# DLRM tower on one core: ACT's relu of an outer-product round in two halves, with the copies of the turned rows between them

## The chip, the cores and the metric

The kernel runs on one core of one Trainium2 chip. The metric is the device time of one launch in microseconds (us), the median of several runs. Engines are named as in the profile: PE (TensorE, matmuls; PEld are its weight loads), DVE (VectorE), ACT (ScalarE), POOL (GpSimd), SP (SyncE, which here only issues DMAs).

## The reference, cut to what matters

Sixteen table rows of 256 numbers are gathered for each of 2048 samples (`e`). Three layers follow. Each forms all products of field f of the embeddings with field g of the layer's own input, contracts the 256 pairs with weights over the 256 columns, adds a bias, applies relu and sums. In the layers k = 1 and 2 the second factor is the same number in every column, so it is an outer product of a projection of the embeddings with the 16 sums of the layer ahead.

```python
for i in range(3):
    z = einsum('bfe,bge->bfge', x, xk).reshape(B, 256, E).swapaxes(1, 2)
    z = einsum('bcl,oc->bol', z, Ws[i]) + bs[i][None, :, None]
    z = sum(relu(z), axis=-1)          # 16 numbers a sample
    outs.append(z)
    xk = broadcast_to(z[:, :, None], (B, F, E))
h = concatenate([*outs, dense_ctx], axis=1)
y = relu(relu(h @ W_top1 + b_top1) @ W_top2 + b_top2) @ W_top3
```

## The kernel before

The batch is cut into 256 tiles of 8 samples x 16 fields, taken two at a time: 128 **slots**. Eight slots make a **group** of 128 samples; there are 16 groups. I write p0 to p7 for a slot's number modulo 8. The slots 12 to 15 are p4 to p7 of the first round of the pattern, and from slot 20 on every eight slots are alike.

In each slot s every engine does this, in an order written out by hand:

- POOL gathers the rows of slot s+4 (two indirect DMAs) and multiplies small parts of the products of slot s+1.
- PE transposes the rows of slot s+2 into PSUM (`turn`, L653; it waits for the DVE products of slot s), then sums the products of slot s with the weights (`sum_pairs`, L675), then does what the slot has beside that: a projection (p3, L753), an **outer round** (p4, p5 for k=0, p0, p1 for k=1; L743), a **fold** (p6 for k=0, p3 for k=1; L774), or parts of the final layers.
- ACT copies the turned rows of slot s+2 from PSUM to SBUF (`take_turned`, two copies, L489 and L490), takes relu and a sum of slot s's pairs (`relu_pairs`, L517 and L521), and squares the fields of slot s+2 (L507).
- DVE multiplies the shifted fields of slot s (`products`, L232; it waits for ACT's two copies of slot s, made two slots earlier), and in p3 it adds relu of the second round of k=1 (L389), in p4 it transposes the projection and reduces a fold, in p0 it reduces the other fold, in p1 the pairs' sums.

An outer round is four matmuls j = 0 to 3 that fill the four banks of `outer_ps`, 128 x 2048 numbers. ACT turns a round into `relu_k` with one instruction over all four banks (`relu_round`, L528), at the head of the slot after the round, ahead of the copies. Of the two rounds q = 0 and 1 of k=1 DVE takes the second. The next round may not write `outer_ps` before that, so PE waits on `outer_relu` ahead of the round q = 1. The fold sums `relu_k` over fields: for k=0 the 16 matmuls of round q = 0 and the 16 of q = 1 (each shown as two passes in the trace, so 64), behind one wait for the relu of q = 1; it writes bank 0 (k=0) or 1 (k=1) of `outer_ps`.

The 16 sums of layer 0 pass through DRAM: ACT's copy (L542, p2), four small writes and one read of 256 KB on SP's queue (L265, L269) into `z_wide`. PE waits for that read inside `sum_pairs` of p4, three matmuls before its end, ahead of the outer round.

## Time and profile before

| | us |
|---|---|
| median of 3 runs (572.27 to 573.78) | 572.27 |
| the profiled execution | 569.55 |
| its span | 567.6 |
| one group of eight slots in the steady part | 33.23 |

The profile gives for each engine its busy time, for each instruction its start and length, and for each idle stretch what ended it. A start and the start of the next instruction on the same engine are the safer pair: lengths on ACT and DVE overlap by a tenth or so of a microsecond, and the ends of matmuls are modelled.

### The profile page before, as it was taken

How to read it: one execution, taken by the hardware profiler on the slowest of the kernel's cores; microseconds unless marked ns; L12 is line 12 of the kernel's file. 1: busy time of each engine (PE TensorE's matmuls, PEld its weight loads, DVE VectorE, ACT ScalarE, POOL GpSimd, SP SyncE). 2: the span in 40 equal slices, each digit the busy share in tenths (PEclk: the TensorE clock that was granted, in tenths of full speed). 3: DMA queues.
4: the chain of work that ended last, by engine and by line, in shares of the span. 5: the costliest groups of instructions: out<-in, count | busy, mean ns of one | idle time of the engine just before them, and what ended most of it. 6: DMA issues, size and time to landing. Idle time of an engine off the chain costs nothing.

```text
span 567.6 us, 17941 instructions
## 1 busy us (share of the span) xinstructions
PE 533.4 (94%) x7520; PEld 302.9 (53%) x7520; DVE 524.3 (92%) x257; ACT 408.5 (72%) x1219; POOL 458.4 (81%) x547
## 2 busy tenths in 40 slices
PE   2776999999999999999999999999999999999997
PEld 1433454555556555554655555555555555555466
DVE  4899899999999999999999999999999999999853
ACT  3566775868878686786868778786877868687743
POOL 6898999998989889897898979888897988988100
PEclk9999999999999999999999999999999999999999
DMA  3622323232232323223232322323222232322000
GB/s 89 176 69 73 86 68 89 65 93 63 64 84 68 85 59 92 60 67 86 58 94 58 83 70 65 83 63 91 61 71 79 61 86 66 86 59 71 14 2 2
DMA packets 27969, 40.57 MB, mean 71 GB/s; under 512 B 16880, under 2 KB 17264, under 8 KB 27888
## 3 DMA queue, kind: packets, MB, share of 16 engines
q0 software_dynamic: 12288, 33.57, 20.8%
q1 hardware_dynamic: 15600, 5.86, 4.2%
q8 instruction: 58, 0.95, 0.7%
q14 instruction: 23, 0.19, 0.1%
HBM read 38.75 MB, written 0.66 MB: 69 GB/s over the span
## 4 chain that ended last, share of the span: by engine, by line
ACT 32%; PE 28%; DVE 17%; issue 14%; POOL 6%; DMA 2%; SPq 0%; ACTq 0%; DVEq 0%; POOLq 0%
ACT relu_k L528 13%; PE sum_ps L675 12%; DVE prods L232 11%; ACT relu L517 6%; DVE relu_k L389 5%; PE outer_ps L774 5%; ACT prods L507 4%; POOL emb L285 4%; PE turn_ps L653 3%; ACT emb_t L489 3%; ACT h L559 2%; PE sum_ps L690 2%; ACT own L521 2%; POOL prods L298 1%; PE outer_ps L743 1%
## 5 line engine op out<-in xcount | busy, mean ns | idle before, releaser
L232 DVE TENSOR_TENSOR prods<-turn_ps,emb_t 128x3248 f32<-128x3248 f32 (+2 forms) x126 | 447.9, 3572 | 11.9 <-ACT emb_t L490 11.8
L285 POOL DMA_INDIRECT emb<-tables,rows_sb x256 | 252.0, 984 | 44.2 <-issue 38.0
L675 PE MATMUL sum_ps<-prods,w_sb 128*32 128x272 f32 x4096 | 264.8, 397 | 3.0 <-POOL prods L232 2.7
L675 PEld LDWEIGHTS sum_ps<-prods,w_sb 128*32 128x32 f32 x4096 | 121.3, 110 | 100.0 <-issue 13.3
L517 ACT ACTIVATE relu<-sum_ps,bias_twice 128x120 f32<-128x120 f32 x256 | 92.8, 378 | 96.5 <-PE sum_ps L675 96.4
L298 POOL TENSOR_TENSOR prods<-emb_t 128x256 f32<-128x256 f32 x128 | 95.2, 744 | 29.2 <-ACT emb_t L490 27.2
L489 ACT COPY emb_t<-turn_ps 128x512 f32<-128x512 f32 (+1 forms) x126 | 76.4, 606 | 36.5 <-PE turn_ps L653 36.4
L653 PEld LDWEIGHTS turn_ps<-ident_sb,emb 128*128 128x128 f32 x502 | 53.0, 141 | 74.2 <-DVE prods L232 53.3
L653 PE MATMUL turn_ps<-ident_sb,emb 128*128 128x128 f32 x502 | 83.2, 288 | 9.6 <-DVE prods L232 7.8
L232 POOL TENSOR_TENSOR prods<-emb_t 128x224 f32<-128x224 f32 (+1 forms) x128 | 89.9, 703 | 2.3
L528 ACT ACTIVATE relu_k<-outer_ps,bias_k 128x2048 f32<-128x2048 f32 x44 | 88.3, 2006 | 0.3 <-PE outer_ps L743 0.3
L507 ACT ACTIVATE prods<-emb_t 128x512 f32<-128x512 f32 x128 | 84.8, 663 | 0.2
L743 PE MATMUL outer_ps<-z_wide,proj_b 32*128 32x512 f32 x488 | 70.1, 643 | 1.2 <-DVE relu_k L421 0.6
L517 ACT ACTIVATION_READ_ACCUMULATOR relu<-sum_ps,bias_twice 128x1 f32 x256 | 55.8, 218 | 0.0
L774 PEld LDWEIGHTS outer_ps<-relu_k,fold_sb 128*32 128x32 f32 x1536 | 41.7, 110 | 20.5 <-ACT relu_k L528 10.7
L774 PE MATMUL outer_ps<-relu_k,fold_sb 128*32 128x128 f32 x1536 | 48.0, 274 | 4.0 <-ACT relu_k L528 3.7
L490 ACT COPY emb_t<-turn_ps 128x256 f32<-128x256 f32 (+1 forms) x126 | 51.6, 409 | 0.0
L521 ACT ACTIVATE own<-sum_ps,bias_sb 128x32 f32<-128x32 f32 x128 | 39.5, 309 | 0.0
L743 PEld LDWEIGHTS outer_ps<-z_wide,proj_b 32*128 32x128 f32 x488 | 20.0, 190 | 27.8 <-issue 19.5
L389 DVE SCALAR_TENSOR_TENSOR relu_k<-outer_ps,bias_less,relu_k 128x2048 f32<-128x2048 f32 x14 | 32.8, 2342 | 0.0
L753 PE MATMUL outer_ps<-emb_t,wp_sb 128*32 128x512 f32 x256 | 30.5, 592 | 0.0
L690 PE MATMUL sum_ps<-h,w_sb 128*128 128x128 f32 x216 | 28.6, 275 | 0.0
(81 smaller groups left out, 249.4 us busy)
## 6 DMA issues: line engine op xcount, KB each, us to landing
emb<-tables,rows_sb POOLq DMA_INDIRECT x256, 2.8
z_wide<-z_spread SPq DMA_DIRECT2D x15, 256.0 KB, 2.7
z_spread<-z_cat SPq DMA_DIRECT2D x60, 2.0 KB, 1.7
w_sb<-w_top SPq DMA_DIRECT2D x1, 512.0 KB
z_spread<-z_wide SPq DMA_DIRECT2D x2, 256.0 KB
w_sb<-w_top SPq DMA_DIRECT2D x1, 256.0 KB
ids_sb<-ids_t SPq DMA_DIRECT2D x1, 129.0 KB, 2.0
z_cat<-dense_b SPq DMA_DIRECT2D x1, 128.0 KB
```

The source lines that it names most:

```text
L232: eng.tensor_tensor(out, every, shifted, ALU.mult).then_inc(done, 1)
L285: nc.gpsimd.indirect_dma_start(out=emb[:, k % EMB_RING, t * E:(t + 1) * E], out_offset=None, in_=tables, in_offset=bass.IndirectOffsetOnAx ...
L298: nc.gpsimd.tensor_tensor(prod_blocks(k)[:, :, SHIFTS * F:], x[:, :, 0:SHIFTS], x[:, :, SHIFTS:F], ALU.mult).then_inc(prods_other[k % PROD ...
L389: nc.vector.scalar_tensor_tensor(out=second, in0=outer_ps[:].rearrange("p j n -> p (j n)"), scalar=bias_less[:], in1=first, op0=ALU.max, o ...
L489: nc.scalar.copy(out[:, half:, 0:F], src[:, half:, :]).then_inc(emb_t_ready, 1)
L507: nc.scalar.square(prod_blocks(k)[:, :, 0:F], emb_blocks(k)[:, :, 0:F]).then_inc(prods_other[k % PRODS_RING], 1)
L517: nc.scalar.activation(relu0[:, k % 2, t, :], sum_ps[:, k % 2, t * PAIRS + F:(t + 1) * PAIRS], ACT.Relu, bias=bias_twice[:, 0:1], scale=2. ...
L528: nc.scalar.activation(relu_k[:, k, q, :, :].rearrange("p j n -> p (j n)"), outer_ps[:].rearrange("p j n -> p (j n)"), ACT.Relu, bias=bias ...
L653: last = nc.tensor.transpose(out[:, i * P:(i + 1) * P], emb[:, k % EMB_RING, i * P:(i + 1) * P], ident_sb[:])
L675: last = nc.tensor.matmul(sum_ps[s * 2 * F:(s + 1) * 2 * F, k % 2, 0:SUM_COLS], w_sb[:, c, odd, :], x[:, c, 2 * s + odd, :, :], start=c == ...
L743: return nc.tensor.matmul(out, y[:, k, q * HALF_F * F:(q + 1) * HALF_F * F], z_wide[j * R:(j + 1) * R, k, :, :].rearrange("p q n -> p (q n ...
L774: last = nc.tensor.matmul(out[j * R:(j + 1) * R, :], fold_sb[:], relu_k[:, k, q, j, n * P:(n + 1) * P], start=first and n == 0, stop=final ...
```

## The change

ACT's relu of a round becomes two instructions over two banks each (`half` 0 and 1). Half 0 stands where the relu stood, half 1 behind the two copies of the turned rows. The counter `outer_relu` goes up by 2 for a round, also where DVE takes it. PE waits in the second round q = 1 twice, ahead of j = 0 for half 0 and ahead of j = 2 for half 1 of the round before, and takes j in the order 0, 1, 2, 3 for both k. The fold of k=0 waits for half 0 of round 1 ahead of round 0's matmuls, and for half 1 ahead of round 1's.

```diff
+RELUS = 2
...
-                dve.wait_ge(outer_relu, n)
+                dve.wait_ge(outer_relu, RELUS * n)
...
-            def relu_round(k, g, q):
+            def relu_round(k, g, q, half):
 
                 act.wait_ge(outer_done, ROUND_NO[k, g, q] + 1)
                 at_least(act, fold_done[k], g)
-                nc.scalar.activation(relu_k[:, k, q, :, :].rearrange("p j n -> p (j n)"), outer_ps[:].rearrange("p j n -> p (j n)"),
+                j = slice(half * 2, half * 2 + 2)
+                nc.scalar.activation(relu_k[:, k, q, j, :].rearrange("p j n -> p (j n)"), outer_ps[:, j, :].rearrange("p j n -> p (j n)"),
                                      ACT.Relu, bias=bias_k[:, k:k + 1]).then_inc(outer_relu, 1)
...
             def outer_round(k, g, q):
 
-                if q > 0:
-                    pe.wait_ge(outer_relu, ROUND_NO[k, g, q])
-                for j in ((2, 3, 0, 1), (0, 1, 2, 3))[k]:
+                for j in ((2, 3, 0, 1), (0, 1, 2, 3))[k] if q == 0 else range(J):
+                    if q > 0 and j % 2 == 0:
+                        pe.wait_ge(outer_relu, RELUS * ROUND_NO[k, g, q] - 1 + j // 2)
...
             def fold(k, g):
 
-                pe.wait_ge(outer_relu, ROUND_NO[k, g, TURNS - 1] + 1)
                 for q in range(k, TURNS):
+                    pe.wait_ge(outer_relu, RELUS * ROUND_NO[k, g, TURNS - 1] + q + 1)
                     last = add_round(k, q, outer_ps[:, FOLD_BANK[k], 0:P], q == k, q == TURNS - 1)
...
                 if slot - 1 in ROUND_AT and (ROUND_AT[slot - 1][0], ROUND_AT[slot - 1][2]) != (1, 1):
-                    relu_round(*ROUND_AT[slot - 1])
+                    relu_round(*ROUND_AT[slot - 1], 0)
...
                     take_turned(ahead)
+                if slot - 1 in ROUND_AT and (ROUND_AT[slot - 1][0], ROUND_AT[slot - 1][2]) != (1, 1):
+                    relu_round(*ROUND_AT[slot - 1], 1)
```

ACT, from the squares at the end of p4 to the relu of pairs in p6 (steady part). Before, the relu over 2048 columns stands ahead of the two copies:

```order
L507 ACTIVATE prods<-emb_t 128x32x16
L528 ACTIVATE relu_k<-outer_ps,bias_k 128x2048
L489 COPY emb_t<-turn_ps 128x32x16
L490 COPY emb_t<-turn_ps 128x32x8
L517 ACTIVATE relu,own<-sum_ps,bias_twice 128x120 x2
L521 ACTIVATE own<-sum_ps,bias_sb 128x2x16
L546 ACTIVATE h<-sum_ps,bias_all 128x128
L507 ACTIVATE prods<-emb_t 128x32x16
L528 ACTIVATE relu_k<-outer_ps,bias_k 128x2048
L489 COPY emb_t<-turn_ps 128x32x16
L490 COPY emb_t<-turn_ps 128x32x8
L517 ACTIVATE relu,own<-sum_ps,bias_twice 128x120 x2
```

The same place in the changed kernel, from its first half on:

```order
L530 ACTIVATE relu_k<-outer_ps,bias_k 128x1024
L490 COPY emb_t<-turn_ps 128x32x16
L491 COPY emb_t<-turn_ps 128x32x8
L530 ACTIVATE relu_k<-outer_ps,bias_k 128x1024
L518 ACTIVATE relu,own<-sum_ps,bias_twice 128x120 x2
L522 ACTIVATE own<-sum_ps,bias_sb 128x2x16
L548 ACTIVATE h<-sum_ps,bias_all 128x128
L508 ACTIVATE prods<-emb_t 128x32x16
L530 ACTIVATE relu_k<-outer_ps,bias_k 128x1024
L490 COPY emb_t<-turn_ps 128x32x16
L491 COPY emb_t<-turn_ps 128x32x8
L530 ACTIVATE relu_k<-outer_ps,bias_k 128x1024
```

Both copies moved ahead of half of the relu; nothing else changed places.

PE, the fold of k=0 in p6 and what follows it. Before, one wait stands ahead of all 32 matmuls (a wait is shown with the instruction that it holds):

```order
L774 MATMUL outer_ps<-relu_k,fold_sb 32x128 [waits outer_relu]
L774 MATMUL outer_ps<-relu_k,fold_sb 32x128 x31
L653 MATMUL turn_ps<-ident_sb,emb 128x128 [waits prods_dve]
L653 MATMUL turn_ps<-ident_sb,emb 128x128
L653 MATMUL turn_ps<-ident_sb,emb 128x128 [waits h0_ready]
```

The same place after the change:

```order
L778 MATMUL outer_ps<-relu_k,fold_sb 32x128 [waits outer_relu]
L778 MATMUL outer_ps<-relu_k,fold_sb 32x128 x15
L778 MATMUL outer_ps<-relu_k,fold_sb 32x128 [waits outer_relu]
L778 MATMUL outer_ps<-relu_k,fold_sb 32x128 x15
L657 MATMUL turn_ps<-ident_sb,emb 128x128 [waits prods_dve]
```

No matmul moved; a second wait stands in the middle of the fold.

## Rows read from the trace of the kernel before

**Rows 1.** The page: busy time by engine; the group of ACT's relu.
```profile
PE 533.4 (94%) x7520; PEld 302.9 (53%) x7520; DVE 524.3 (92%) x257; ACT 408.5 (72%) x1219; POOL 458.4 (81%) x547
...
L528 ACT ACTIVATE relu_k<-outer_ps,bias_k 128x2048 f32<-128x2048 f32 x44 | 88.3, 2006 | 0.3 <-PE outer_ps L743 0.3
```

**Rows 2.** Busy time by stretch, one steady group (relu_add of DVE to the next).
```profile
core 0: us, PE busy (x) PEld busy (x) DVE busy (x) ACT busy (x) POOL busy (x), PEclk, DMA share, GB/s
...
319.00:352.23 33.23, 32.72 (x473) 18.68 (x466) 32.30 (x17) 25.39 (x76) 28.74 (x35) 1.00 0.26 74
```

**Rows 3.** Waits in total: who waited for whom, us, times, longest.
```profile
DVE prods L232 <- ACT emb_t L490: 11.8, 27, 0.6
...
PE turn_ps L653 <- DVE prods L232: 7.8, 21, 0.9
...
PE outer_ps L774 <- ACT relu_k L528: 3.7, 12, 0.3
...
PEld sum_ps L675 <- DMA z_wide<-z_spread: 1.1, 2, 0.6
```

**Rows 4.** Timeline of PE: start, length, instruction, idle before it and its releaser.
```profile
124.85 0.66 PE L653 MATMUL turn_ps<-ident_sb,emb 128*128 128x128 f32 x4 [0.20 <-DVE prods L232]
...
300.79 2.04 PE L675 MATMUL sum_ps<-prods,w_sb 128*32 128x272 f32 x32
...
303.13 1.95 PE L774 MATMUL outer_ps<-relu_k,fold_sb 128*32 128x128 f32 x64 [0.29 <-ACT relu_k L528]
...
305.01 0.66 PE L653 MATMUL turn_ps<-ident_sb,emb 128*128 128x128 f32 x4
...
323.57 1.06 PE L774 MATMUL outer_ps<-relu_k,fold_sb 128*32 128x128 f32 x32
...
324.84 0.66 PE L653 MATMUL turn_ps<-ident_sb,emb 128*128 128x128 f32 x4 [0.21 <-DVE prods L232]
...
524.27 0.66 PE L653 MATMUL turn_ps<-ident_sb,emb 128*128 128x128 f32 x4 [0.21 <-DVE prods L232]
```

**Rows 5.** Timeline of PE in the first two groups: folds without a wait.
```profile
70.45 1.96 PE L774 MATMUL outer_ps<-relu_k,fold_sb 128*32 128x128 f32 x64
...
72.34 0.66 PE L653 MATMUL turn_ps<-ident_sb,emb 128*128 128x128 f32 x4
...
91.39 1.06 PE L774 MATMUL outer_ps<-relu_k,fold_sb 128*32 128x128 f32 x32
...
92.38 0.66 PE L653 MATMUL turn_ps<-ident_sb,emb 128*128 128x128 f32 x4
```

**Rows 6.** Timeline of ACT and DVE in one steady group, 301 to 316 us.
```profile
301.03 2.04 ACT L528 ACTIVATE relu_k<-outer_ps,bias_k 128x2048 f32<-128x2048 f32 x1
302.88 0.67 ACT L489 COPY emb_t<-turn_ps 128x512 f32<-128x512 f32 x1
...
303.61 0.47 ACT L517 ACTIVATE relu<-sum_ps,bias_twice 128x120 f32<-128x120 f32 x1
303.86 3.54 DVE L232 TENSOR_TENSOR prods<-turn_ps,emb_t 128x3248 f32<-128x3248 f32 x1 [0.61 <-ACT emb_t L490]
...
310.95 0.44 ACT L490 COPY emb_t<-turn_ps 128x256 f32<-128x256 f32 x1
...
311.64 3.53 DVE L232 TENSOR_TENSOR prods<-turn_ps,emb_t 128x3248 f32<-128x3248 f32 x1
...
315.43 3.66 DVE L232 TENSOR_TENSOR prods<-turn_ps,emb_t 128x3360 f32<-128x3360 f32 x1 [0.25 <-ACT emb_t L490]
```

**Rows 7.** Timeline of ACT at the end, where half relus already stand back to back.
```profile
545.28 1.11 ACT L574 ACTIVATE relu_k<-outer_ps,bias_k 128x1024 f32<-128x1024 f32 x1 [0.74 <-PE outer_ps L743]
546.29 1.11 ACT L574 ACTIVATE relu_k<-turn_ps,bias_k 128x1024 f32<-128x1024 f32 x1
```

**Rows 8.** Timeline of PE in p4 of one group; landing of the read into `z_wide`.
```profile
259.25 2.68 PE L675 MATMUL sum_ps<-prods,w_sb 128*32 128x272 f32 x32
...
DMA to landing us min/median/max: 2.5/2.7/3.4
```

More of the change, by code:

```diff
@@ L389, in relu_add @@
                 nc.vector.scalar_tensor_tensor(out=second, in0=outer_ps[:].rearrange("p j n -> p (j n)"), scalar=bias_less[:],
-                                               in1=first, op0=ALU.max, op1=ALU.add).then_inc(outer_relu, 1)
+                                               in1=first, op0=ALU.max, op1=ALU.add).then_inc(outer_relu, RELUS)
             def reduce_fields(k, g, src):
@@ L673, in sum_pairs @@
                                 if (c, odd, s) == (1, 1, 3) and (g := group_at(k, PROJ)) is not None and g > 0:
-                                    pe.wait_ge(outer_relu, ROUND_NO[1, g - 1, TURNS - 1] + 1)
+                                    pe.wait_ge(outer_relu, RELUS * (ROUND_NO[1, g - 1, TURNS - 1] + 1))
                                 last = nc.tensor.matmul(sum_ps[s * 2 * F:(s + 1) * 2 * F, k % 2, 0:SUM_COLS], w_sb[:, c, odd, :],
@@ L812, in _ @@
                 if slot == STEPS - 1:
-                    pe.wait_ge(outer_relu, ROUND_NO[0, PREV, 1] + 1)
+                    pe.wait_ge(outer_relu, RELUS * (ROUND_NO[0, PREV, 1] + 1))
                     hidden1(LAST - 2, h1_banks)
```

## The prediction

> **What bounds the kernel now.** I read the busy table first. PE is busy for 94% of the span and DVE for 92%, ACT for 72% [rows 1]. In one steady group of 33.23 us PE is busy for 32.72 and DVE for 32.30 [rows 2]. So PE has 0.51 us of idle time in a group, and whatever DVE or ACT may save, the kernel can't gain much more than that: some 14 groups x 0.5 = 7 us.
>
> Next I read which waits make up those 0.51 us. The waits name two places, and the timeline shows them in each steady group [rows 3, 4]. **Place A** is the fold of k=0 in p6: PE is idle for 0.29 until ACT's relu of round 1 ends (12 times, 3.7 us in all). **Place B** is the turn in p4: PE is idle for 0.21 until DVE's products end. Of its 21 rows 13 lie in the steady part, 8 slots apart from 124.85 to 524.27 (13 x 0.21 = 2.7 of the 7.8 us); the others lie before the first outer round. 0.29 + 0.21 is the whole of PE's idle time.
>
> DVE waits too, for ACT's copies: 0.61 in p0, where the copies stand behind the relu of round 1, and 0.25 in p3, behind that of k=1 [rows 6]. Those are the waits that the change addresses. They cost time only through place B.
>
> **Place B, a gain.** Without a wait, a fold of k=1 and the turn behind it lie 0.99 us apart (91.39 to 92.38) [rows 5]; now they lie 1.27 apart (323.57 to 324.84) [rows 4]. If DVE is no longer late, PE gains 0.28. Does DVE come early enough? The wait of 0.25 in p3 vanishes, since the copies no longer stand behind the second half of the relu: they come 2.04 - 1.11 = 0.9 us earlier. The 0.61 in p0 vanishes or shrinks as well, but DVE can't keep all of it, because its products of p2 start at 311.64 and their copies end at 311.39 [rows 6]: only 0.25 may be kept there. So DVE is earlier at the end of p4 by 0.25 to 0.5, and PE by its own path could start at 324.56. It will be DVE's 324.8 less 0.25 at least, 324.55: in time, all the more as PE itself comes later by the loss below. I take the whole 0.28.
>
> **Place A, a loss.** What has to end before the second part of the fold is now: half 0, both copies, half 1. The row of the relu over 2048 columns takes 2.04 and lets the next instruction start after 1.85 (301.03 to 302.88); the two copies let the next start after 0.73 (302.88 to 303.61) [rows 6]. Half relus stand in the trace already, at its end: length 1.11, next start after 1.01 [rows 7].
>
> - Splitting costs ACT 2 x 1.01 - 1.85 = 0.17 a round. The chain from the round in p4 to the fold in p6 is ACT's alone, without idle time, so the split of round 0 pushes round 1 by +0.17.
> - In round 1, half 1 ends 1.01 + 0.73 + 1.11 = 2.85 after half 0's start, where the whole relu ended after 2.04: +0.81, and up to +0.87 if its length is stretched by 0.06 as that of the 2048-column row against the others (2.04 against 1.98 to 2.01). I take +0.87.
> - Behind this end stood all 64 passes of the fold, and the next turn came 1.88 later (303.13 to 305.01) [rows 4]. Now half of them stand behind it, 0.99 by the fold of 32 [rows 5]: -0.89.
> - Sum: 0.17 + 0.87 - 0.89 = **+0.15 a group**. The first part of the fold hides in the wait: PE's sums end about 302.76 (300.79 + 1.97), later by the delay at most, and 0.9 more for 32 passes ends at about 303.8, while half 1 ends at 303.07 + 0.17 + 0.87 = 304.11.
>
> In short, the fold loses by the copies what it gains by starting with round 0, and pays the split on top. The bounds of this term: 0.05 (fold part 0.94 instead of 0.99, no stretch) and, with one more stop of PE of 0.3 at each side of the new wait, about 0.45. The nearest row for restarting after a wait speaks for the low end: the fold of 64 passes takes 1.88 to the next turn behind a wait and 1.89 without one [rows 4, 5].
>
> **What is hidden.** The new wait ahead of j = 2 in round q = 1 (p5) may stop PE for 0.1 to 0.2: half 1 of round 0 ends about then. That delays PE's sums of p6, which end well ahead of the new end of half 1, so it costs nothing; without that cover it would be 0.1 to 0.2 a group. In p1 half 1 ends before PE reaches the round. DVE's and POOL's waits for `outer_relu` and the copies are all earlier or have slack. ACT is some 0.3 us later with the pairs' relu of p6 and catches up at p7, where it waited for PE's turn.
>
> **The sum.** Place B: 13 x -0.28 = -3.6. Place A: 13 x +0.15 = +1.95 (14 folds; the first group has DVE far ahead of everything and absorbs it). In two groups PE also waited for the read into `z_wide`, 1.1 us in all [rows 3]; in one of them the sums of p4 took 2.68 instead of 2.04 [rows 8]. That read starts from PE's work in p2, and a turn that comes earlier only waits longer there, so the gain of place B is lost in those two: +0.6. At the end, where ACT's last round is followed by no copies, the split stays in the path: +0.17. Total: -3.6 + 1.95 + 0.6 + 0.17 = **-0.9 us**. This is against the profiled execution's own 569.55 (span 567.6). The runs' median is 572.27, 2.7 more; I put the difference on that: 572.27 - 0.9, rounded to **571.4 us**. A change of 0.3%, 1.7 us, is about what a measurement can tell from none.
>
> **A rule weighed.** A relu over 2048 columns lasts 2.01 on average and one over 1024 lasts 1.11 [rows 1, 7], and the pipeline hides part of each. The Trainium skill, "ScalarE: Activation LUTs", section "Rules for kernel authors", budgets about 0.3 us for each ACTIVATE and 0.83 ns for each element. By that the split would cost 0.3 a round (estimate), not 0.17, and the trace disagrees with it by what back-to-back starts show. By its price the loss of place A would come to 0.15 + 0.13 for round 0 and 0.13 for round 1, some 0.4 a group, and the sum to about +2.5 us.
>
> **Rivals.**
>
> *The fold restarts dearly (slower).* Two waits in the middle of matmul runs, where there was none, keep weights from being loaded ahead. If each adds 0.15, place A costs 0.45, more than place B gives: 13 x (0.45 - 0.28) + 0.8 = +3.0, so 575.3. It decides from a loss of 0.28 - 0.06 = 0.22 a group on. For it: the new stop stands on the chain of ACT and PE in every group. Against: 1.88 against 1.89 above. The Trainium skill, "TensorE: Matmul & The Clock Gate", section "Single matmul latency", gives an isolated matmul a constant of some 0.17 us beside its columns, which a stream hides; it would put this rival at +1.2 us, and no pair of rows here shows such a price.
>
> *The read takes B's place (slower or same).* The read lands 2.5 to 3.4 us after its issue [rows 8], and PE needs it only some 0.9 us after the median landing. If it is late in most groups of the timed runs, place B gives nothing: 13 x 0.15 + 0.17 = +2.1, 574.4.
>
> *It does all it says (faster).* If half 1 ends early enough, or the fold's second part is shorter, place A costs nothing: -3.6 + 0.6 + 0.17 = -2.8, 569.5. If even the idle 0.29 of place A goes, 12 x 0.29 more: 566. For it: the whole idle time of both places is there to be had. Against: two copies of 0.73 stand in that chain, and the fold's first half is worth only 0.89.
>
> *It does nothing.* DVE's saved waits only turn into a wait elsewhere, and the two terms cancel: 572.3. That lies inside the forecast's band.
>
> **How the numbers follow.** The forecast and "nothing" together (570.6 to 574.0): 0.52. The faster rival: 0.28. The slower rivals: 0.20 (dear restart 0.12, read 0.08). The likeliest case's own range is 570.4 to 573.2. The range of 8 in 10 reaches to 568.7 below and 574.7 above, which takes in the bounds 0.05 and about 0.35 of place A. Faster by over 0.3%: 0.28; within: 0.52; slower: 0.20.
>
> **What would show it.** Right: a steady group of about 33.1 us; DVE's waits for the copies (L490, 11.8 us) nearly gone; no idle time of PE at the turn of p4; PE's stop moved from the head of the fold to its middle, about 0.3 to 0.5 long; fold start to next turn of about 2.3. Wrong: PE still waiting for DVE in p4, the turn behind the fold more than 0.28 later in the group, or waits for `z_wide` in more than a few groups. The forecast fails most easily by place A, because it is a small difference of large terms.

## The result, and the profile after

The changed kernel took **582.15 us** (median of 4 runs, 580.73 to 583.28) where the kernel before, on the same chip in the same measurement, took 573.02 (572.27 to 574.23). The ratio is 1.0158, 95% interval 1.0136 to 1.0179: slower by 1.6%. I had forecast 571.4 us, a range of 568.7 to 574.7, and "no difference" as the likeliest outcome. The time is far outside that range. Of all the runs below one, a run of e8, has 579.9 us at a granted clock of 0.951; it is in e8's median and in no ratio.

The profiled execution of the changed kernel has a span of 580.1 us (before 567.6). Its page, the first line of part 1, answers to [rows 1]:

```profile
PE 549.7 (95%) x7520; PEld 313.9 (54%) x7520; DVE 526.4 (91%) x257; ACT 416.2 (72%) x1263; POOL 457.3 (79%) x547
```

PE does the same 7520 matmuls and is busy 16 us longer. Part of that is standing still inside a run, which the row counts as busy: further down, a round of eight passes takes 1.46 us instead of 1.15 and shows no idle time. One group by the windows view, the turn of p5 to the next turn of p5, answers to [rows 2]:

```profile
302.40:336.44 34.04, 33.62 (x466) 19.46 (x466) 32.42 (x16) 25.98 (x80) 28.67 (x34) 1.00 0.26 72
```

A group is now 34.04 us long instead of 33.23; twelve groups make 9.7 of the 12.5 us by which the spans differ. The times of the runs, of which both kernels were measured side by side, differ by only 9.1: the two traces turn out to be of different kinds. The granted clock is 1.00 in both groups.

The most useful table is one that no view prints. The timeline has a row for each turn of PE; the distance from one turn to the next is a slot's length. Medians over twelve groups, in us:

| | p0 | p1 | p2 | p3 | p4 | p5 | p6 | p7 | group |
|---|---|---|---|---|---|---|---|---|---|
| before | 3.63 | 4.53 | 2.69 | 5.43 | 4.59 | 4.00 | 4.81 | 3.55 | 33.23 |
| changed | 3.64 | 4.87 | 2.69 | 5.15 | 4.88 | 4.38 | 4.90 | 3.54 | 34.04 |

p3 has lost exactly the 0.28 of place B. p1 costs 0.34 where I had said nothing would happen. From the turn of p4 to the turn of p7, the stretch of place A, PE takes 14.14 instead of 13.40, so place A costs 0.74 and not my 0.15. The single slots in that stretch mislead: p4 is 0.29 longer, but a later section shows that p5 takes this back and that the loss arises in p6. The waits in total, the same view as [rows 3]:

```profile
DVE z_sum L396 <- PE outer_ps L778: 11.2, 14, 1.8
...
PE turn_ps L657 <- DVE prods L233: 5.7, 12, 0.9
...
DVE prods L233 <- ACT emb_t L491: 2.7, 10, 0.4
```

DVE's waits for ACT's copies are nearly gone (11.8 to 2.7), as the steps said. In their place DVE waits 11.2 us for a fold of PE. Before, that wait was 2.8 us, all of it ahead of the steady part.

### The profile page after: what moved, and what is told of

Same layout as the page of the kernel before. It is cut to its first block, busy times and chain, and to the rows that moved or that the text cites. A ratio compares the mean times of both kernels' runs of the same rounds, so it can differ in the third digit from the quotient of the medians.

```text
span 580.1 us, 18039 instructions
## 1 busy us (share of the span) xinstructions
PE 549.7 (95%) x7520; PEld 313.9 (54%) x7520; DVE 526.4 (91%) x257; ACT 416.2 (72%) x1263; POOL 457.3 (79%) x547
## 4 chain that ended last, share of the span: by engine, by line
PE 77%; issue 8%; DVE 7%; DMA 4%; SPq 2%; ACT 1%; POOL 0%; DVEq 0%; ACTq 0%; POOLq 0%
PE sum_ps L679 35%; PE outer_ps L747 11%; PE turn_ps L657 10%; PE outer_ps L778 9%; DVE prods L233 6%; PE outer_ps L757 4%; PE sum_ps L694 3%; PE outer_ps L793 2%; DMA z_wide<-z_spread 2%; DMA z_spread<-z_cat 1%; PE sum_ps L702 1%; PE sum_ps L688 1%; SPq L266 1%; PE outer_ps L694 0%; DMA emb<-tables,rows_sb 0%
## 5 line engine op out<-in xcount | busy, mean ns | idle before, releaser
L679 PE MATMUL sum_ps<-prods,w_sb 128*32 128x272 f32 x4096 | 267.6, 400 | 1.6 <-DMA z_wide<-z_spread 1.4
L530 ACT ACTIVATE relu_k<-outer_ps,bias_k 128x1024 f32<-128x1024 f32 x88 | 102.0, 1161 | 0.0
L747 PE MATMUL outer_ps<-z_wide,proj_b 32*128 32x512 f32 x488 | 81.5, 643 | 0.6 <-DVE relu_k L422 0.6
L778 PE MATMUL outer_ps<-relu_k,fold_sb 128*32 128x128 f32 x1536 | 53.8, 274 | 2.2 <-issue 0.7
L778 PEld LDWEIGHTS outer_ps<-relu_k,fold_sb 128*32 128x32 f32 x1536 | 44.2, 110 | 19.5 <-issue 13.8
L747 PEld LDWEIGHTS outer_ps<-z_wide,proj_b 32*128 32x128 f32 x488 | 27.8, 190 | 30.8 <-issue 24.1
```

Source lines behind the costliest of these rows:

```text
L530: nc.scalar.activation(relu_k[:, k, q, j, :].rearrange("p j n -> p (j n)"), outer_ps[:, j, :].rearrange("p j n -> p (j n)"), ACT.Relu, bia ...
L679: last = nc.tensor.matmul(sum_ps[s * 2 * F:(s + 1) * 2 * F, k % 2, 0:SUM_COLS], w_sb[:, c, odd, :], x[:, c, 2 * s + odd, :, :], start=c == ...
L747: return nc.tensor.matmul(out, y[:, k, q * HALF_F * F:(q + 1) * HALF_F * F], z_wide[j * R:(j + 1) * R, k, :, :].rearrange("p q n -> p (q n ...
L778: last = nc.tensor.matmul(out[j * R:(j + 1) * R, :], fold_sb[:], relu_k[:, k, q, j, n * P:(n + 1) * P], start=first and n == 0, stop=final ...
```

## The experiments

Eighteen runs were made in eight further measurements: the changed kernel three times more, and nine variants, three of them more than once (e5 and e6 do not exist). The kernel before ran beside them in each; a ratio is always to it. For one kernel the medians agree from one measurement to the next only after these are sorted into two kinds, so here is the list first (us):

| measurement | before | changed kernel | variants |
|---|---|---|---|
| 1 | 573.02 | **582.15** | |
| 2 | 570.70 | | e1 576.44, e2 570.74, e3 575.43, e4 572.71 |
| 3 | 570.18 | **571.19** (e10) | e7 570.88, e8 572.11, e9 572.29 |
| 4 | 570.87 | **571.21** (e11) | e12 568.93, e13 573.54 |
| 5 | 572.63 | **582.44** (e14) | |
| 6 | 569.52 | | e15 567.41, e16 571.87 |
| 7 | 569.76 | | e17 568.06 |
| 8 | 569.71 | | e18 568.13 |
| 9 | 573.24 | | e19 571.33, e20 583.95 |

In measurements 1, 5 and 9 the kernel before takes 572.6 to 573.2, in the others 569.5 to 570.9. A single run hardly tells which: those of the one kind lie between 572.14 and 574.67, those of the other between 568.72 and 572.05. I call the first kind **late** and the second **prompt**, for a reason that comes below. Measurements 6 and 9 ran on the same chip, so the kind does not belong to a chip. The only trace of the kernel before, 569.55 us, is of the prompt kind: the slots "before" in this document are prompt ones, and no trace shows what the late kind does to that kernel, which it makes some 2 to 3 us longer.

### Which part costs the time

My first theory was that each step of the change simply costs more than I had said. Three variants undo a part of the change each, and a fourth moves the fold of k=1:

**e1, the split alone.** Both halves stand together ahead of the copies; PE waits once for both.

```diff
                     relu_round(*ROUND_AT[slot - 1], 0)
+                if slot - 1 in ROUND_AT and (ROUND_AT[slot - 1][0], ROUND_AT[slot - 1][2]) != (1, 1):
+                    relu_round(*ROUND_AT[slot - 1], 1)
...
-                    if q > 0 and j % 2 == 0:
-                        pe.wait_ge(outer_relu, RELUS * ROUND_NO[k, g, q] - 1 + j // 2)
+                    if q > 0 and j == 0:
+                        pe.wait_ge(outer_relu, RELUS * ROUND_NO[k, g, q])
...
+                pe.wait_ge(outer_relu, RELUS * (ROUND_NO[k, g, TURNS - 1] + 1))
                 for q in range(k, TURNS):
-                    pe.wait_ge(outer_relu, RELUS * ROUND_NO[k, g, TURNS - 1] + q + 1)
```

> The changed kernel with both halves of the relu ahead of the copies, and with PE waiting for both at the head of the round q = 1 and of the whole fold: only the split is left. Theory A (the split costs 0.17 a round, and the dearest part of the change is where its waits stand): the fold of k=0 comes 2 x 0.17 later in each group, so about 13 x 0.34 = 4.4 over the kernel before: 577.4 us (576 to 579). Rival B (a stop in the middle of a run of matmuls drains PE and costs by itself): no such stop is left, so this kernel shows the split alone, the same 577. Rival C (the split itself costs far more than 0.17 a round): 581 to 583, as the changed kernel.

Measured: 576.44, ratio 1.010 (1.0082 to 1.0117). The slots that changed are p3 (5.58, +0.15) and p6 (5.11, +0.30). ACT's timeline gives the reason, two half relus and what comes next:

```profile
303.76 2.19 ACT L530 ACTIVATE relu_k<-outer_ps,bias_k 128x1024 f32<-128x1024 f32 x2
305.76 0.68 ACT L490 COPY emb_t<-turn_ps 128x512 f32<-128x512 f32 x1
```

Two halves take 2.00 to the next start, the whole relu took 1.85 [rows 6]: a split costs 0.15. Round 1 of k=0 ends behind two splits, hence 0.30 in p6; DVE is late by the one in p1, hence 0.15 in p3. 12 x 0.45 = 5.4 of the 5.7 us. So the split is paid in full wherever nothing is won for it, and my term for it (0.17) was nearly right.

**e2, no stop inside a round.** The changed kernel, but a second round waits for both halves at its head.

```diff
-                    if q > 0 and j % 2 == 0:
-                        pe.wait_ge(outer_relu, RELUS * ROUND_NO[k, g, q] - 1 + j // 2)
+                    if q > 0 and j == 0:
+                        pe.wait_ge(outer_relu, RELUS * ROUND_NO[k, g, q])
```

> The changed kernel, but PE waits once, for half 1, at the head of the round q = 1 (p5 and p1) and not again ahead of j = 2. Theory A (the second half ends only after PE could issue the weight load of j = 2, and from there PE needs the time of a whole round again): the early start of j = 0 and 1 is worth nothing, so this kernel takes as long as the changed one: 582 us, plus or minus 1. Rival B (the stop in mid-round is dear by itself, some 0.2 to 0.3 a time): 4 to 8 us faster than the changed kernel, 575 to 578. A third case (the early start of j = 0, 1 is worth the 0.5 it should be): 5 us or more slower, 587.

Measured: 570.74, ratio 1.0009 (0.9997 to 1.002). It looked as if the stops inside rounds were the whole slowdown. They are not: e10 below has them and is as fast. I had compared 570.74 with the 582.15 of another measurement, and that was the mistake.

**e3, the copies between the halves only in p6.** In p1 and p5 both halves stand ahead of the copies.

```diff
+                if slot - 1 in ROUND_AT and (ROUND_AT[slot - 1][0], ROUND_AT[slot - 1][2]) in ((0, 0), (1, 0)):
+                    relu_round(*ROUND_AT[slot - 1], 1)
...
-                if slot - 1 in ROUND_AT and (ROUND_AT[slot - 1][0], ROUND_AT[slot - 1][2]) != (1, 1):
+                if slot - 1 in ROUND_AT and (ROUND_AT[slot - 1][0], ROUND_AT[slot - 1][2]) == (0, 1):
                     relu_round(*ROUND_AT[slot - 1], 1)
```

> The changed kernel, but the copies stand between the halves only for round 1 of k=0 (p6, ahead of the fold); in p5 and p1 both halves stand ahead of the copies. Theory A: the 0.37 of p5 and the 0.34 of p1 vanish (13 x 0.71 = 9), only the fold's small delay stays: 573 to 574.5 us. Rival B (stops in mid-run): the fold keeps its stop, so 575 to 577. Rival C (the number of ACT instructions): no change from 582.

Measured: 575.43, ratio 1.008 (1.0064 to 1.0097), with p3 at 5.59 and p6 at 5.00. The gain of p3 is absent when the copies of p1 are not between the halves.

**e4, the fold of k=1 ahead of the projection** in p3, and DVE's reduction ahead of its transposition of the projection.

> The changed kernel, but in p3 PE does the fold of k=1 ahead of the projection, and DVE reduces the fold ahead of turning the projection. Theory A (what ate the gain of place B is DVE's reduction, which waits 0.72 us for the fold that is PE's last work of p3, and so PE waits for DVE's products at the turn of p5): DVE starts its products of p5 some 0.25 earlier and PE's wait there goes: 12 x 0.27 = 3.3 faster than the changed kernel, 579 us. Rival: DVE is late there for its own work, or has to wait for the projection for as long: no change, 582, or slower.

Measured: 572.71, ratio 1.0025 (1.0015 to 1.0036). In 6 of 12 groups PE waits in p4 for the read into `z_wide`; the other slots are those of the changed kernel in e10 below. So the reorder wins nothing in a prompt measurement. It did not fall into a late one.

### The same kernel again

**e10, the changed kernel as it is**, with **e7** (a stop inside the round only in p5), **e8** (only in p1) and **e9** (the second gather of a slot issued behind GpSimd's product blocks) beside it.

> The changed kernel as it is, once more. In its trace sums and folds that PE has ended are seen by the other engines 0.3 to 0.6 us late (the second fold's end 0.89 us after its last matmul, where it is 0.31 in the kernel before and in the four variants run so far), and the fold of p6 stops for 0.4 us ahead of its last four weight loads though nothing is waited for. Theory A (this belongs to the program): the time is 1.0136 to 1.018 of the kernel before again, some 579 us where the kernel before takes 571, and the late ends and the stop are in the trace again. Theory B (it belonged to that one chip or that one execution): the late ends are gone, and the time is the stops' own price above the variant that waits at the round's head, 571 to 575 us.

> The changed kernel, but the second round of field k=1 (p1) waits once, at its head, for both halves; the one of k=0 (p5) keeps its stop ahead of j=2. Theory A (each stop pays for itself): p1 is back from 4.87 to 4.53 us, the rest stays, so 12 x 0.34 = 4.1 us are won on the changed kernel: 575 where the kernel before takes 571. Theory B (the late ends come from the stop in p1 and carry all the rest): p4, p5 and p6 come back as well, 571 to 572. Theory C (they come from the stop in p5): only p1 changes and the second fold's end is still seen 0.89 us after its last matmul, 575.

> The changed kernel, but the second round of field k=0 (p5) waits once, at its head; the one of k=1 (p1) keeps its stop ahead of j=2. Theory A (each stop pays for itself): p5 and p6 together go from 9.28 to 9.04 us, p1 stays at 4.87 and p4 at 4.88: 12 x 0.24 = 2.9 us won on the changed kernel, 576 where the kernel before takes 571. Theory B (the late ends come from the stop in p1): as theory A, late ends still there. Theory C (they come from the stop in p5): p4 comes back to 4.54 too, and p1 alone keeps a loss of up to 0.34: 571 to 575.

> The changed kernel with the two last steps of a slot swapped on GpSimd: the second gather of a slot is issued behind the product blocks and no longer ahead of them, some 0.7 us later; everything else as in the changed kernel. Theory D (a gather's landing just ahead of the end of PE's sums holds PE's signal back): the landings move away from the ends of the sums, sums_done in p0 is seen at 2.67 us again instead of 3.10, and the time comes back to 571 to 575 where the kernel before takes 571. If the landing has nothing to do with it, the late ends stay and the time is that of the changed kernel, 579, or up to 4 us more if the product blocks or the gathers now come too late.

Measured: e10 **571.19**, ratio 1.0012 (0.9999 to 1.0026), and by slot 3.64, 4.53, 2.69, 5.15, 4.53, 4.70, 4.36, 3.54, a group of 33.14. The changed kernel is not 1.6% slower here; it can't be told from the kernel before. e7 (1.0011) and e8 (1.0025) have the same slots to 0.02 us, so in a prompt measurement it makes no difference whether PE waits for half 1 at a round's head or inside it. e9 is at 1.003.

**e11 and e14, the same kernel a third and a fourth time.**

> The changed kernel as it is, a third time, on whatever chip it falls. Theory B (the 9 us of the first measurement lay with that chip or those executions, not with the program): about 571 us, at most 0.3% above the kernel before, the second fold's end seen 0.32 us after its last matmul starts. Theory A' (the program has two patterns and falls into one or the other): in one measurement of three or so it is at 1.013 to 1.018 again, with late ends in its trace.

> The changed kernel as it is, a fourth time, to see how often the pattern of the first measurement comes back. If it lay with that chip or those executions: 570 to 573 us again, p1 at 4.53 us and p4 at 4.53. If the program falls into one of two patterns by itself: 579 to 583 in one of some three measurements, with p1 at 4.87 and p4 at 4.88.

Measured: e11 571.21, ratio 1.0013 (1.0003 to 1.0023, so 0.1% slower by a hair); e14 **582.44** in two runs, ratio 1.0172 (1.0137 to 1.0206). The slots of e14 are those of the first trace again (p1 4.87, p4 4.86, p5 4.40, p6 4.91). So the program has two times, and which one it gets is settled outside it.

**What differs in a late measurement.** The four traces of measurements 1, 5 and 9 have in common that PE's signals reach the other engines late. I took each matmul that raises a semaphore between 120 and 530 us and the time at which the trace records the rise. In e10 and e12 none of some 320 comes more than 0.08 us later than the usual delay for its kind. In the four late traces 44 to 60 of some 290 do, by 0.36 to 0.42 us on average, and in one kernel at the same places of every group. (The trace of the kernel before has none.) Two places in the timelines, the sums of p0 and the fold of k=1. First the changed kernel in measurement 1:

```profile
315.82 2.04 PE L679 MATMUL sum_ps<-prods,w_sb 128*32 128x272 f32 x32
...
318.33 0.36 ACT L518 ACTIVATE relu<-sum_ps,bias_twice 128x120 f32<-128x120 f32 x1 [0.28 <-PE sum_ps L679]
...
330.56 1.06 PE L778 MATMUL outer_ps<-relu_k,fold_sb 128*32 128x128 f32 x32
...
332.31 0.29 DVE L396 TENSOR_REDUCE z_sum<-outer_ps 128x32 f32<-128x128 f32 x1 [0.72 <-PE outer_ps L778]
```

Then e10, the same kernel in measurement 3:

```profile
309.66 2.04 PE L679 MATMUL sum_ps<-prods,w_sb 128*32 128x272 f32 x32
...
311.77 0.40 ACT L518 ACTIVATE relu<-sum_ps,bias_twice 128x120 f32<-128x120 f32 x1
...
324.08 1.22 PE L778 MATMUL outer_ps<-relu_k,fold_sb 128*32 128x128 f32 x32
...
325.36 0.29 DVE L396 TENSOR_REDUCE z_sum<-outer_ps 128x32 f32<-128x128 f32 x1
```

PE takes the same 2.04 us for the sums in both, but ACT starts 2.51 us after their start instead of 2.11. DVE's reduction starts 1.75 after the fold's start instead of 1.28. In the late traces half of the records of DMA completions are missing as well (2,640 to 2,770 records instead of some 5,500), and so are some of PE's own signals. The late signals stand behind more DMA completions, of all queues, than the others: some 12 to 17 in the microsecond ahead against 7 to 9. That is a correlation; it is not shown that the completions hold the signals back, nor that they do not: the recording of the trace, which loses records in these very traces, is a rival that no run here tests. e9 was meant to test the gathers' part in it, and so was its repetition e16:

> The changed kernel with the second gather of each slot issued behind GpSimd's product blocks, once more. Where signals come on time: 1.003 of the kernel before. Where they come late: if a gather's landing just ahead of PE's signal holds the signal back (theory D), moving half of the landings changes the pattern: sums_done in p0 at 2.67 us again or late at other places, and 573 to 578 instead of 582. If the landings have nothing to do with it, 582 or more.

Both fell into prompt measurements (1.003 and 1.0034), so that theory stays untested.

**From a late signal to the lost time.** In p1 of measurement 1, ACT and then PE:

```profile
318.33 0.36 ACT L518 ACTIVATE relu<-sum_ps,bias_twice 128x120 f32<-128x120 f32 x1 [0.28 <-PE sum_ps L679]
...
319.71 1.12 ACT L530 ACTIVATE relu_k<-outer_ps,bias_k 128x1024 f32<-128x1024 f32 x1
...
321.44 1.16 ACT L530 ACTIVATE relu_k<-outer_ps,bias_k 128x1024 f32<-128x1024 f32 x1
...
322.32 1.46 PE L747 MATMUL outer_ps<-z_wide,proj_b 32*128 32x512 f32 x8
...
323.72 0.65 PE L657 MATMUL turn_ps<-ident_sb,emb 128*128 128x128 f32 x4
```

And in e10:

```profile
314.87 1.20 ACT L530 ACTIVATE relu_k<-outer_ps,bias_k 128x1024 f32<-128x1024 f32 x1
...
316.16 1.15 PE L747 MATMUL outer_ps<-z_wide,proj_b 32*128 32x512 f32 x8
...
317.24 0.66 PE L657 MATMUL turn_ps<-ident_sb,emb 128*128 128x128 f32 x4
```

In e10 half 1 ends at 316.07, 0.09 us before PE starts the round: my sentence "in p1 half 1 ends before PE reaches the round" holds, by 0.09 us. The copies between the halves have put the end of a round's relu 0.9 us later, and that was all the slack there was. When the sums of p0 are signalled 0.4 late, ACT's pairs' relu, half 0, the copies and half 1 are all 0.4 late; half 1 ends at 322.60, and PE, which started the round at 322.32, stands still inside it and loses 0.34. In p4 the late end of the fold of k=1 does the same to DVE: its reduction starts 0.5 later than in e10, and so as late as in the kernel before, where DVE is busy until then. The turn waits for DVE's products. A row like the one at 324.84 in [rows 4] now stands one slot later in the group:

```profile
336.44 0.66 PE L657 MATMUL turn_ps<-ident_sb,emb 128*128 128x128 f32 x4 [0.29 <-DVE prods L233]
```

Place B's wait has moved from the turn of p4 to the turn of p5. But it costs nothing there. The round of p5 has to wait for half 1 of the round before in any case, and the medians, counted from the turn of p4, come together again:

| us from the turn of p4 | turn p5 | turn p6 | half 1 ends | fold starts | its second part starts | turn p7 |
|---|---|---|---|---|---|---|
| e10, prompt | 4.53 | 9.23 | 12.53 | 11.68 | 12.58 | 13.59 |
| changed, measurement 1 | 4.88 | 9.22 | 12.51 | 11.67 | 12.57 | 14.14 |

The whole difference of 0.55 arises in the second part of the fold. In p6 of measurement 1 and then of e10:

```profile
308.84 1.23 ACT L530 ACTIVATE relu_k<-outer_ps,bias_k 128x1024 f32<-128x1024 f32 x1
...
309.22 2.54 PE L778 MATMUL outer_ps<-relu_k,fold_sb 128*32 128x128 f32 x64
...
311.69 0.66 PE L657 MATMUL turn_ps<-ident_sb,emb 128*128 128x128 f32 x4
```

```profile
303.23 1.24 ACT L530 ACTIVATE relu_k<-outer_ps,bias_k 128x1024 f32<-128x1024 f32 x1
...
303.61 1.99 PE L778 MATMUL outer_ps<-relu_k,fold_sb 128*32 128x128 f32 x64
...
305.53 0.66 PE L657 MATMUL turn_ps<-ident_sb,emb 128*128 128x128 f32 x4
```

From the end of half 1 to the turn it is 1.62 us in the first and 1.06 in the second. The weight loads show where PE stands still, again measurement 1 and e10:

```profile
309.00 1.92 PEld L778 LDWEIGHTS outer_ps<-relu_k,fold_sb 128*32 128x32 f32 x60
311.31 0.18 PEld L778 LDWEIGHTS outer_ps<-relu_k,fold_sb 128*32 128x32 f32 x4 [0.40 <-issue]
```

```profile
303.38 1.94 PEld L778 LDWEIGHTS outer_ps<-relu_k,fold_sb 128*32 128x32 f32 x64
```

A stop of 0.4 us lies some 28 passes behind the second wait, where the program has no wait. I found no cause for it. It is in 13 of the first 14 folds of k=0 in measurement 1, in 12 of e14 and in 13 of e20 (below), and in none of the prompt traces. So of the 0.90 us by which a group of the changed kernel is longer in measurement 1 than in e10, 0.34 arise in p1 by the late signal and 0.55 in the fold, most of it by this stop.

### The two places apart

**e12, place B alone:** only the round of p1 is split, with the copies between its halves. Both rounds of k=0 have one relu over 2048 columns ahead of the copies, the fold of k=0 waits once, and second rounds wait once and take j in the order of the kernel before.

```diff
+                if k == 0:
+                    if half == 0:
...
+                        nc.scalar.activation(relu_k[:, k, q, :, :].rearrange("p j n -> p (j n)"),
...
+                                             ACT.Relu, bias=bias_k[:, k:k + 1]).then_inc(outer_relu, RELUS)
+                    return
...
-                for j in ((2, 3, 0, 1), (0, 1, 2, 3))[k] if q == 0 else range(J):
-                    if q > 0 and j % 2 == 0:
-                        pe.wait_ge(outer_relu, RELUS * ROUND_NO[k, g, q] - 1 + j // 2)
+                for j in ((2, 3, 0, 1), (0, 1, 2, 3))[k]:
+                    if q > 0 and j == (2, 0)[k]:
+                        pe.wait_ge(outer_relu, RELUS * ROUND_NO[k, g, q])
...
+                pe.wait_ge(outer_relu, RELUS * (ROUND_NO[k, g, TURNS - 1] + 1))
                 for q in range(k, TURNS):
-                    pe.wait_ge(outer_relu, RELUS * ROUND_NO[k, g, TURNS - 1] + q + 1)
```

> Only the first round of field k=1 (its relu stands in p1) is split with the copies between; both rounds of k=0 have the one relu over 2048 columns ahead of the copies, and the fold of k=0 waits once, as before. By my steps place B's gain alone: p3 at 5.15 us instead of 5.43, p4 to p6 as before (4.59, 4.00, 4.81), a group of 32.95 and 12 or 13 x 0.28 = 3.4 to 3.6 us less than the kernel before: 567 where that takes 570.5. If DVE needs the copies of p5 and p6 early as well to be in time in p4, the gain is smaller or nothing (570.5). If the read into z_wide takes its place in some groups, 568 to 569.

**e13, place A alone:** the rounds of k=0 as in the changed kernel, the round of p1 with its one relu ahead of the copies.

> The other half of the change: both rounds of k=0 split with the copies between, the stop in p5 and the second wait in the fold; the round of k=1 has its one relu ahead of the copies. By my steps place A's loss alone: p5 and p6 together 8.96 us (prediction) or 9.05 (as the other runs show it) instead of 8.81, p3 at 5.43: 12 to 14 x 0.15 to 0.25 = 1.8 to 3.5 us more than the kernel before, 572.4 to 574 where that takes 570.5. If DVE's earlier copies in p6 and p7 alone are enough for place B, p3 is 5.15 here too and the time is that of the kernel before.

Measured: e12 568.93, ratio **0.9961** (0.9947 to 0.9976); e13 573.54, ratio **1.0048** (1.0032 to 1.0065). The product, 1.0009, is the changed kernel's 1.0013 in the same measurement. By slot:

| prompt | p3 | p4 | p5 | p6 | group |
|---|---|---|---|---|---|
| before | 5.43 | 4.59 | 4.00 | 4.81 | 33.23 |
| e12, place B alone | 5.15 | 4.53 | 4.01 | 4.86 | 32.95 |
| e13, place A alone | 5.43 | 4.59 | 4.65 | 4.36 | 33.43 |
| e10, both | 5.15 | 4.53 | 4.70 | 4.36 | 33.14 |

The places add up, as the sum had them. In e12's timeline the fold of k=1 and the turn behind it are 0.98 us apart without a wait, as in [rows 5], and the fold of k=0 waits as before:

```profile
302.56 1.95 PE L786 MATMUL outer_ps<-relu_k,fold_sb 128*32 128x128 f32 x64 [0.34 <-ACT relu_k L531]
304.45 0.66 PE L665 MATMUL turn_ps<-ident_sb,emb 128*128 128x128 f32 x4
...
323.01 1.06 PE L786 MATMUL outer_ps<-relu_k,fold_sb 128*32 128x128 f32 x32
323.99 0.66 PE L665 MATMUL turn_ps<-ident_sb,emb 128*128 128x128 f32 x4
```

In e13's the wait of place B is still there:

```profile
325.47 1.06 PE L786 MATMUL outer_ps<-relu_k,fold_sb 128*32 128x128 f32 x32
326.74 0.66 PE L665 MATMUL turn_ps<-ident_sb,emb 128*128 128x128 f32 x4 [0.21 <-DVE prods L233]
```

e12 is a better kernel than both. Does it hold where signals are late? It ran four times more.

> Place B alone once more (only the round of p1 split, one wait ahead of the fold of k=0, the second rounds wait once). Where the chip gives PE's signals on time: 0.996 of the kernel before, as in the first measurement. Where it gives them late, as where the changed kernel took 582: if the late signals come with any copies between halves, about 1.01; if they need the stops inside a round or a fold, which this kernel has none of, 0.995 to 1.0 there too.

> Place B alone, a third time. The kernel before, timed beside it, tells the chip: about 570 where signals come on time, 572.6 where they come late. On time: 0.996 to 0.997 again. Late: about 1.01 if the copies between the halves of the round in p1 bring the late signals, 0.995 to 1.0 if they need the stops of place A.

Measured: e15 0.9966 (0.9954 to 0.9979), e17 0.9963 (0.9943 to 0.9984), and e18, the same once more, 0.997 (0.9946 to 0.9995), all prompt. The last time it fell into a late measurement, beside the kernel of e2:

> Place B alone, a last time: 0.996 to 0.997 of the kernel before on a chip where that takes about 570; on one where it takes 572.6, about 1.01 if the copies between the halves bring the late signals, 0.995 to 1.0 if the stops of place A do.

> The changed kernel with one wait at the head of each second round, once more: 1.001 of the kernel before on a chip where that takes 570. On one where it takes 572.6: about 1.016 like the changed kernel if the fold's second wait or the copies bring the late signals, about 1.0 to 1.005 if the stops inside the rounds do.

Measured: e19 571.33, ratio **0.9962** (0.9944 to 0.998); e20 583.95 in two runs, ratio **1.0178** (1.0142 to 1.0214). e20 clears the stops inside the rounds: without them the loss is all there. e19 has late signals too (60 of 282), but at other places, and its fold of k=1 is on time. DVE's reduction in e19, then in e20:

```profile
324.81 1.06 PE L786 MATMUL outer_ps<-relu_k,fold_sb 128*32 128x128 f32 x32
...
326.10 0.25 DVE L396 TENSOR_REDUCE z_sum<-outer_ps 128x32 f32<-128x128 f32 x1
```

```profile
330.50 1.06 PE L778 MATMUL outer_ps<-relu_k,fold_sb 128*32 128x128 f32 x32
...
332.22 0.29 DVE L396 TENSOR_REDUCE z_sum<-outer_ps 128x32 f32<-128x128 f32 x1 [0.70 <-PE outer_ps L778]
```

1.29 after the fold's start without a wait, against 1.72. In e19 the end of the fold of k=0 is signalled 0.97 late, in front of slack, and of the slots only p1 (4.65, +0.12) and p6 (4.91) are longer than in e12. Its fold of k=0, which waits once, has no such stop in any group; e20's, with the second wait, has it as the changed kernel does. So in a late measurement the loss needs place A's part of the change. Whether it needs the early copies in p5 and p6 or the fold's second wait wasn't separated, and whether place A does it without place B isn't known either: place A alone did not fall into a late measurement, and place B alone did only once.

## Why the prediction was wrong

- **The step that failed is the one I made in a single sentence, "The runs' median is 572.27, 2.7 more; I put the difference on that".** The profiled execution, 569.55, lay outside the range of the runs (572.27 to 573.78). I treated the 2.7 us as an offset. It was the sign that the runs and the trace came from executions of different kinds: 569.55 is a prompt time and 572.27 a late one. Every step was then worked out from a prompt trace and applied to late runs. What the late runs showed in its place is +9.1 us, and by the late trace two terms make it: the stop in p1, which I had put at nothing (+0.34 a group), and the fold's second part, where the next turn comes 1.63 behind half 1's end and not 1.06, so that place A costs 0.74. With place B, 12 x (0.34 + 0.74 - 0.28) = +9.6 against the prompt trace of the kernel before. That the kind makes the difference is shown by the same kernel at 571.2 and at 582.4; what makes the late kind is open.
- **Place B, -0.28 a group: right.** p3 went from 5.43 to 5.15 in every trace with the copies of p1 between the halves, prompt or late. e12 turns it into 0.3 to 0.4%. Late, DVE is not early enough for the turn of p5, since it waits for the fold's signal, and p4 is 0.29 longer; p5 hides that. "DVE comes early enough" had a margin that I never put against a delay in a signal.
- **Place A, +0.15 a group: nearly right in prompt measurements, wrong in late ones.** From the turn of p4 to that of p7 e10 takes 13.59, before 13.40: +0.19. Term by term: half 0 of round 1 starts 0.15 later than the whole relu did, against the turn of p4 (I had 0.17); half 1 ends 1.07 later than that ended (1.04); behind its end come 1.06 us to the next turn instead of 1.94 (-0.88, I had -0.89). What is missing is half 1's length, 1.24, where I had 1.11 and a stretch of 0.06. Late, the term of -0.88 shrinks to -0.31, by the stop inside the fold, and place A costs 0.74.
- **"In p1 half 1 ends before PE reaches the round": true by 0.09 us in a prompt trace, false in a late one, +0.34 a group.** I gave the sentence no number. With the prompt trace's own rows it would have read "by 0.1 us", and its loss would have been a rival with a price. The wait inside the round gives no further margin: in e10's trace the first passes of all four matmuls of that round start within 0.02 us, so j = 2 is due as soon as j = 0 is.
- **The stop ahead of j = 2 in p5, "0.1 to 0.2, hidden".** PE's slot p5 is 0.70 longer in e10 (4.70 against 4.00), not 0.1 to 0.2, and yet it is hidden as I said: e2, which stops at the head, has the same 4.70. The slot only takes what p6 no longer waits. The sign that I named, a stop of 0.3 to 0.5 in the fold's middle and 2.3 from the fold's start to the next turn, did not come: in e10 it is 1.92 (303.61 to 305.53). PE reaches the fold 0.86 ahead of half 1's end, just the time of its first part, so the cover was there with next to nothing to spare.
- **The sum.** Had all measurements been prompt, the forecast's case was the right one: 571.19 and 571.21 against a forecast of 571.4, though that agreement is partly luck, since the kernel before was 570.2 to 570.9 there and not 572.3. Against it the change is +0.3 to +1.0 us, not -0.9. The spans of e10 and before, 568.8 and 567.6, close so: steady groups 12 x -0.09 = -1.1; longer waits for the read into `z_wide` in p4 +1.5 (3 groups, I had +0.6 in two); start of the pattern +0.45; end +0.3 (I had +0.17). The rival "the read takes B's place" is real but small, 0.3 to 1.5 us in e10, e11 and e12.
- **The dear restart** was the rival on the right side. In prompt measurements it is refuted: e7 and e8 cost nothing by their stops, and behind the fold's second wait the time is -0.88 where I had -0.89. In late ones taking the stops out of the rounds saves nothing (e20), but the fold's stop lies behind the very wait that this rival spoke of and appears only in kernels that have it. It is 0.55 a group where the rival had 0.3, and without a cause it can be put neither for the rival nor against it. The rule that I weighed, 0.3 us for each ACTIVATE (the Trainium skill, "ScalarE: Activation LUTs", "Rules for kernel authors"), is twice what e1 shows for a split, 0.15.

## What to carry to other kernels

Put the profiled execution's own time against the range of the runs first; if it lies outside, the trace may show another kind of execution than the one that is timed, as it did here, and then a difference of slots can't be carried over. Give each "hidden" its margin in us and ask what happens if a signal comes 0.4 us late: a change that moved an end from 1 us of slack to 0.1 cost nothing in one measurement and 0.34 us in every group of the next. And take a change apart before judging it: here one third of it, the copies between the halves in p1 alone, is worth 0.3 to 0.4% in all five measurements, one of them late, and the rest costs 0.5% where it was run, in a prompt one.

## What the runs showed of the hardware

- One program on one core has two times. The kernel before takes 569.5 to 570.9 or 572.6 to 573.2, the changed kernel 571.2 or 582.2 to 582.4, and the profiled executions of both kinds have a granted clock of 0.996 to 1.0; one chip gave both kinds in two measurements. Within a measurement all runs at a granted clock of 0.996 or more are of one kind.
- In the longer kind PE's semaphore signals are recorded 0.1 to 1.0 us later at fixed places of each group, and half of the DMA completion records are missing. In the three late traces whose fold of k=0 has a second wait, PE stands still for 0.4 us some 28 passes behind it in 12 or 13 of 14 folds; in the late trace without that wait it does not. The Trainium skill, "Perfetto Trace Analysis", section "Per-instruction lifecycle: what the profiler-reported window actually captures", says that a signal's way to the other engines lies outside an instruction's profiled window and that PE's end is a model. The traces agree: PE's row of the sums has the same 2.04 us in both kinds, and the delay shows only as the wait of ACT. What makes the signal 0.4 us late stays open.
- Two relus over 1024 columns instead of one over 2048 cost ACT 0.15 us.
